# Graph attention network on one core: one StreamTranspose and four small writes for a row, three of four masked tiles scaled by ScalarE, the last batches in halves, and a new order of steps

## The chip, the cores and the metric

The kernel runs on one core of a Trainium2 chip. The core has five engines that work side by side: TensorE (PE, matmuls and transposes), VectorE (DVE), ScalarE (ACT), GpSimd (POOL) and SyncE (SP, which here only starts DMAs). Each takes its instructions in the order in which the program gives them, and waits at semaphores. The metric is the time of one execution on the device, in microseconds.

## The reference, cut to what matters

x has 16 batches of 512 nodes with 128 features; adj is a 512 x 512 matrix of edges. Two blocks follow one another, the first with two attention layers, the second with one:

```
def gat(inp, adj_mask, W, a):
    h = inp @ W
    f1, f2 = h @ a[:F, 0], h @ a[F:, 0]
    e = leaky_relu(f1[:, :, None] + f2[:, None, :], 0.2)
    e = where(adj_mask > 0, e, -9e15)        # not in the first layer
    return elu(softmax(e, axis=2) @ h)

h = relu(layernorm(x))                       # 16 x 512 x 128
o = relu(h @ mlp1_w + mlp1_b)                # 256 wide
o = elu(gat(o, None, W_fc, a_fc)) + o        # layer 1, 256 wide, no mask
o = relu(o @ mlp2_w + mlp2_b)                # 128 wide
o = relu(elu(gat(o, adj, W_hand, a_hand)) + o)   # layer 2, masked
x = x + o
h = relu(layernorm(x))
x = x + elu(attention(h, adj, W, a) @ (h @ W))   # layer 3, masked
```

## The kernel before, in words

A batch is cut into four tiles (C = 4) of 128 nodes. For each batch, numbered 0 to 15, the kernel does the same chain of steps, and each step has a name: `load`, `stats1`, `root1`, `norm1`, `turn1` (layer norm and transposing), `mlp1_0`, `mlp1_1`, `h1_0` to `h1_3`, `max1`, `args1`, `row1`, `prob1_0` to `prob1_3`, `att1_0` to `att1_3`, `elu1_0`, `elu1_1`, `z_0`, `z_1` (layer 1), `mlp2`, then the masked layer 2 (`h2`, `max2`, `args2`, `row2`, `prob2`, `att2`, `elu2`, `turn_o2`, `x1`, `norm2`, `root2`, `turn2`) and the masked layer 3 (`h3`, `max3`, `args3`, `row3`, `prob3`, `att3`, `elu3`, `result`). Step `x1` makes the residual x + o, `norm2` its statistics and normalised tiles, which `turn2` on TensorE transposes for `h3`.

The softmax's weights are never computed as an exponential of a sum over 512 x 512 pairs. exp(leaky_relu(f1 + f2)) is the larger of two products, so ScalarE takes exponentials of three short columns (`args`, L728, into `square`), and an attention tile is max(row x scale, bound), then cut by the mask with a minimum. For that, one of the columns (one value for each of the 512 nodes) has to lie along the free axis and be the same on all 128 partitions: the *row*. In batches 0 to 2 and 13 to 15 (which of them depends on the layer) TensorE spreads it by transposing a broadcast column and ScalarE copies it (L735). In the other 36 cases VectorE transposes the 128 x 32 tile `square` in four blocks of 32 x 32 into `square_t` with 32 partitions (`turn_row`, L1019), SyncE writes four lines of 512 B to DRAM (L570), waits for that, and loads the row broadcast to 128 partitions (L580).

The attention tiles of a masked layer are made in `prob_alone` and `prob_scaled`. VectorE makes tiles 0 and 1 alone, with a TensorScalar each (multiply, max; L1041) and then a TensorTensor each (min with the mask; L1046). For tiles 2 and 3 ScalarE multiplies the row (L744), and VectorE takes max and min in one ScalarTensorTensor (L1053). The attention's matmuls on TensorE (L1281 for layer 1, L1364 for the masked ones) wait for these tiles; a reciprocal on VectorE (L1090, L1097) and a scaled copy on ScalarE (L775, L785) read their bank. elu is an Exp on ScalarE (L793; twice in layers 1 and 2, L797) and a ScalarTensorTensor on VectorE (L1105); `x1` is two more (L954, L961), `result` one (L1120), each of 512 columns.

What each engine does when is written out by hand: `ORDER` holds for each of the five engines the list of its steps with their batches, and several batches are under way at once in different layers. Matmuls go through eight banks of PSUM in turn, in TensorE's order, so a matmul also waits until the bank of eight fillings before has been read. Most buffers have two slots, for even and odd batches. At the end a general version of the network stands behind a flag (`guard`, `flag`), which runs only where the scores leave a range; it does not run with these inputs.

Of the kernel before, what the change touches and what calls it, by code (L numbers as in the profile page):

```python
# [6 lines left out]
P = 128  # L7
# [12 lines left out]

WARM = (10, 12)
# [7 lines left out]
        load.0 load.1 weights load.2 load.3 load.4 load_again.0 load.5 load.6 load.7 load.8 load.9 row1.3  # L29
        load_again.1 load.10 row1.4 row1.5 load.11 row2.2 load_again.2 row2.3 load.12 row3.1 result.0 load.13  # L30
        row1.6 row2.4 load_again.3 row1.7 row2.5 load.14 row3.2 row3.3 load_again.4 result.1 load.15 row1.8
        row2.6 load_again.5 row1.9 row2.7 row3.4 row1.10 row3.5 result.2 load_again.6 result.3 result.4
        load_again.7 load_again.8 result.5 row2.8 row3.6 row3.7 row1.11 row2.9 load_again.9 result.6 row2.10
        load_again.10 row1.12 result.7 row3.8 row2.11 row1.13 row3.9 load_again.11 result.8 row1.14 row3.10
        row2.12 result.9 load_again.12 row3.11 row1.15 load_again.13 result.10 result.11 row3.12 load_again.14
        load_again.15 result.12 result.13 result.14 result.15
    """,
    "gpsimd": """
        max1.0 max1.1 max1.2 max2.0 max1.3 max2.1 max1.4 max3.0 max1.5 max2.2 max2.3 max3.1 max1.6 max2.4
        max1.7 max2.5 max3.2 max3.3 max1.8 max2.6 max2.7 max1.9 max3.4 max1.10 max3.5 max2.8 max3.6 max2.9  # L40
        max3.7 max1.11 max2.10 max1.12 max3.8 max2.11 max3.9 max1.13 max1.14 max3.10 max2.12 max2.13 max3.11
        max1.15 max2.14 max3.12 max3.13 max2.15 max3.14 max3.15 guard
    """,
    "scalar": """
        weights root1.0 turn_w1 turn_w23 root1.1 turn1.0 turn1.1 root1.2 mlp1_0.0 mlp1_1.0 h1_0.0 h1_1.0
        mlp1_0.1 h1_2.0 root1.3 h1_3.0 turn1.2 mlp1_1.1 turn1.3 h1_0.1 h1_1.1 mlp1_0.2 h1_2.1 args1.0 h1_3.1
        root1.4 masks_0 mlp1_1.2 masks_1 row1.0 args1.1 masks_2 masks_3 root1.5 row1.1 att1_0.0 att1_1.0
        elu1_0.0 turn1.4 att1_2.0 root1.6 h1_0.2 h1_1.2 att1_3.0 elu1_1.0 h1_2.2 h1_3.2 att1_0.1 att1_1.1
        turn1.5 mlp1_0.3 root1.7 elu1_0.1 mlp1_1.3 att1_2.1 mlp2.0 att1_3.1 h2_0.0 root1.8 args1.2 h2_1.0
        h1_0.3 elu1_1.1 h1_1.3 h1_2.3 args2.0 h1_3.3 args1.3 row2.0 prob2_2.0 row1.2 mlp2.1 prob2_3.0 h2_0.1  # L50
        mlp1_0.4 att2_0.0 turn1.6 att2_1.0 elu2.0 h2_1.1 root1.9 mlp1_1.4 att1_0.2 args2.1 att1_1.2 row2.1
        elu1_0.2 h1_0.4 prob2_2.1 prob2_3.1 att1_2.2 root1.10 root2.0 h1_1.4 h1_2.4 h1_3.4 turn2.0 args1.4
        att1_3.2 elu1_1.2 att2_0.1 att1_0.3 att2_1.1 att1_1.3 h3_0.0 elu2.1 elu1_0.3 att1_2.3 att1_3.3 elu1_1.3
        h3_1.0 att1_0.4 args3.0 mlp1_0.5 mlp1_1.5 row3.0 att1_1.4 h1_0.5 root2.1 h1_1.5 prob3_2.0 prob3_3.0
        elu1_0.4 mlp1_0.6 h1_2.5 h1_3.5 att1_2.4 args1.5 att1_3.4 mlp2.2 turn2.1 elu1_1.4 mlp2.3 turn1.7 h3_0.1
        h2_0.2 h2_1.2 args2.2 att1_0.5 h2_0.3 mlp2.4 h2_1.3 att1_1.5 elu1_0.5 att1_2.5 args2.3 att1_3.5 h3_1.1
        prob2_2.2 elu1_1.5 att3_0.0 mlp1_1.6 turn1.8 att3_1.0 prob2_3.2 root1.11 args3.1 mlp1_0.7 prob2_2.3
        elu3.0 h1_0.6 h1_1.6 h1_2.6 h1_3.6 prob2_3.3 mlp2.5 turn1.9 mlp1_1.7 att2_0.2 mlp1_0.8 prob3_2.1
        prob3_3.1 h2_0.4 h1_0.7 args1.6 h2_1.4 att2_1.2 h1_1.7 h1_2.7 root1.12 elu2.2 args2.4 h1_3.7 args1.7
        root2.2 att3_0.1 att3_1.1 turn2.2 att2_0.3 h2_0.5 att2_1.3 h2_1.5 prob2_2.4 args2.5 prob2_3.4 elu2.3  # L60
        elu3.1 att1_0.6 h3_0.2 att1_1.6 elu1_0.6 prob2_2.5 att2_0.4 att1_2.6 mlp1_1.8 prob2_3.5 att2_1.4
        att1_3.6 turn1.10 h1_0.8 h3_1.2 h1_1.8 elu2.4 elu1_1.6 turn2.3 root2.3 args3.2 att2_0.5 h1_2.8 att2_1.5
        h3_0.3 h3_1.3 att1_0.7 att1_1.7 prob3_2.2 root1.13 args3.3 mlp1_0.9 h1_3.8 mlp2.6 elu2.5 elu1_0.7
# [1419 lines left out]
```

## Time and profile before

| | us |
|---|---|
| time, median of 3 runs | 476.24 (475.93 to 479.42) |
| the profiled execution: its own time | 479.25 |
| the profiled execution: its span, first to last instruction | 477.5 |
| TensorE busy | 435.4 (91%), 2601 matmuls |
| VectorE busy | 387.4 (81%), 1371 instructions |
| ScalarE busy | 306.8 (64%), 739 instructions |
| GpSimd busy | 26.6 (6%) |
| mean granted TensorE clock | 0.984 of full speed |

Busy time is the time in which at least one instruction of the engine runs; the rest of the span it waits. Where an engine had been idle, the profile names what released it.

### The profile page before, as it was taken

How to read it: one execution, taken by the hardware profiler on the slowest of the kernel's cores; microseconds unless marked ns; L12 is line 12 of the kernel's file. 1: busy time of each engine (PE TensorE's matmuls, PEld its weight loads, DVE VectorE, ACT ScalarE, POOL GpSimd, SP SyncE). 2: the span in 40 equal slices, each digit the busy share in tenths (PEclk: the TensorE clock that was granted, in tenths of full speed). 3: DMA queues.
4: the chain of work that ended last, by engine and by line, in shares of the span. 5: the costliest groups of instructions: out<-in, count | busy, mean ns of one | idle time of the engine just before them, and what ended most of it. 6: DMA issues, size and time to landing. Idle time of an engine off the chain costs nothing. (4 is left out here: it accounts for less than half of the span.)

```text
span 477.5 us, 8672 instructions
## 1 busy us (share of the span) xinstructions
PE 435.4 (91%) x2601; PEld 366.6 (77%) x2601; DVE 387.4 (81%) x1371; ACT 306.8 (64%) x739; POOL 26.6 (6%) x53
## 2 busy tenths in 40 slices
PE   6899999999999899999989998999899997978582
PEld 6678778877779787878878867888788896967472
DVE  6796588586699988799998886997896999888862
ACT  2566747757477486947676863886746594866552
POOL 0000000000001000010000010001001000100000
PEclk9999999999999999999999998999999999999977
DMA  6210120001122201230132022102210303020001
GB/s 209 67 46 23 45 66 1 25 0 44 46 68 67 68 24 44 68 85 19 53 110 71 22 69 66 46 22 68 77 34 25 88 1 84 29 68 22 23 1 49
DMA packets 32394, 24.42 MB, mean 51 GB/s; under 512 B 1595, under 2 KB 27222, under 8 KB 32342
## 3 DMA queue, kind: packets, MB, share of 16 engines
q1 hardware_dynamic: 30960, 22.23, 16.1%
q10 hardware_dynamic: 1382, 1.58, 1.0%
q8 instruction: 22, 0.36, 0.3%
q14 instruction: 30, 0.25, 0.2%
HBM read 19.54 MB, written 4.27 MB: 50 GB/s over the span
## 5 line engine op out<-in xcount | busy, mean ns | idle before, releaser
L1364 PE MATMUL bank<-ext,prob 128*128 128x129 f32 x1024 | 129.4, 280 | 7.4 <-DVE prob L1053 6.1
L1364 PEld LDWEIGHTS bank<-ext,prob 128*128 128x128 f32 x1024 | 123.6, 194 | 15.0 <-DVE prob L1053 8.8
L1281 PE MATMUL bank<-ext,prob 128*128 128x257 f32 x512 | 118.1, 381 | 2.3 <-DVE prob L1031 2.0
L1281 PEld LDWEIGHTS bank<-ext,prob 128*128 128x128 f32 x512 | 94.6, 190 | 18.8 <-issue 3.7
L1270 PE MATMUL bank<-wfc_sb,o_t 128*128 128x259 f32 x256 | 64.1, 386 | 1.3 <-ACT o_t L682 1.3
L1270 PEld LDWEIGHTS bank<-wfc_sb,o_t 128*128 128x128 f32 x256 | 46.8, 193 | 10.1 <-issue 2.9
L1105 DVE SCALAR_TENSOR_TENSOR u<-e,y 128x512 f32<-128x512 f32 x64 | 43.8, 688 | 11.7 <-ACT e L797 7.3
L785 ACT ACTIVATE y<-bank,recip 128x128 f32<-128x128 f32 x128 | 39.0, 369 | 21.5 <-DVE recip L1097 20.6
L609 POOL PARTITION_ALL_REDUCE fmax<-fmax_col x48 | 26.0, 545 | 432.2 <-DVE fmax_col L983 432.2
L775 ACT ACTIVATE y<-bank,recip 128x256 f32<-128x256 f32 x64 | 29.8, 474 | 30.9 <-DVE recip L1090 30.3
L1053 DVE SCALAR_TENSOR_TENSOR prob<-prob,square,mask_t 128x512 f32<-128x512 f32 x64 | 47.0, 746 | 2.7 <-ACT prob L744 2.5
L793 ACT ACTIVATE e<-y,minus_one 128x512 f32<-128x512 f32 x64 | 46.3, 724 | 0.9
L744 ACT ACTIVATE prob<-row,square 128x512 f32<-128x512 f32 x64 | 44.7, 724 | 0.9 <-DMA row<-row_scratch 0.7
L1046 DVE TENSOR_TENSOR prob<-prob,mask_t 128x512 f32<-128x512 f32 x64 | 41.3, 688 | 0.0
L1041 DVE TENSOR_SCALAR prob<-row,square 128x512 f32<-128x512 f32 x64 | 32.0, 544 | 4.9 <-ACT row L735 4.7
L797 ACT ACTIVATE e<-e,minus_one 128x512 f32<-128x512 f32 x48 | 34.8, 724 | 1.6
L1019 DVE STREAM_TRANSPOSE square_t<-square 32x32 f32<-32x32 f32 x144 | 28.6, 198 | 7.1 <-ACT square L728 3.4
L690 ACT ACTIVATE ext<-bank 128x259 f32<-128x259 f32 x64 | 23.3, 386 | 16.4 <-PE bank L1270 15.5
L1031 DVE TENSOR_SCALAR prob<-row,square 128x512 f32<-128x512 f32 x64 | 32.4, 540 | 1.6 <-DMA row<-row_scratch 1.5
L1299 PE MATMUL bank<-z_t,w_sb 128*128 128x512 f32 x64 | 30.6, 600 | 2.2 <-DVE z_t L1112 1.5
L1261 PE MATMUL bank<-normed_t,w_sb 128*128 128x512 f32 x64 | 32.0, 596 | 0.4 <-ACT y L785 0.4
L728 ACT ACTIVATE square<-args 128x12 f32<-128x12 f32 x48 | 10.1, 210 | 32.8 <-DVE args L1004 17.8
(95 smaller groups left out, 535.0 us busy)
## 6 DMA issues: line engine op xcount, KB each, us to landing
row<-row_scratch SPq DMA_DIRECT2D x36, 256.0 KB, 3.2
x_in<-in_x SPq DMA_DIRECT2D x16, 256.0 KB, 2.8
x_res<-in_x SPq DMA_DIRECT2D x16, 256.0 KB, 4.1
out<-y_out SPq DMA_DIRECT2D x16, 256.0 KB, 2.8
adj_sb<-in_adj ACTq DMA_DIRECT2D x1, 1024.0 KB, 5.5
row_scratch<-square_t SPq DMA_DIRECT2D x36, 2.0 KB
wfc_sb<-in_L_gnn_W_fc ACTq DMA_DIRECT2D x1, 256.0 KB, 3.8
w_sb<-in_L_gnn_mlp_w SPq DMA_DIRECT2D x1, 128.0 KB, 4.0
```

The costliest lines, as they stand in the source:

```text
L744: nc.scalar.activation(L.prob_of(b)[:, t], L.row[:, b.slot], ACT.Copy, scale=L.buv[:, b.slot, 2, t:t + 1]).then_inc(s.scaled_row.sem, 1)
L785: nc.scalar.activation(L.y[:, c], filled[:, e * (D + 3):e * (D + 3) + D], ACT.Copy, bias=1.0, scale=L.recip[:, b.slot, c:c + 1]).then_inc( ...
L793: nc.scalar.activation(L.e[:, r], L.y[:, r], ACT.Exp, bias=minus_one[:]).then_inc(s.exp.sem, 1)
L797: nc.scalar.activation(L.e[:, r], L.e[:, r], ACT.Exp, bias=minus_one[:]).then_inc(s.exp2.sem, 1)
L1031: nc.vector.tensor_scalar(gat1.prob_of(b)[:, t], gat1.row[:, b.slot], gat1.buv[:, b.slot, 2, t:t + 1], gat1.buv[:, b.slot, 1, t:t + 1], AL ...
L1041: nc.vector.tensor_scalar(p[:, t], L.row[:, b.slot], L.buv[:, b.slot, 2, t:t + 1], L.buv[:, b.slot, 1, t:t + 1], ALU.mult, ALU.max).then_i ...
L1046: nc.vector.tensor_tensor(p[:, t], p[:, t], mask_t[:, t], ALU.min).then_inc(s.prob_ready.sem, 1)
L1053: nc.vector.scalar_tensor_tensor(out=p, in0=p, scalar=L.buv[:, b.slot, 1, t:t + 1], in1=mask_t[:, t], op0=ALU.max, op1=ALU.min).then_inc(s ...
L1105: nc.vector.scalar_tensor_tensor(out=L.u[:, r], in0=L.e[:, r], scalar=1.0, in1=L.y[:, r], op0=ALU.min, op1=ALU.max).then_inc(s.u.sem, 1)
L1270: last = nc.tensor.matmul(filled[:, 0:H + 3], o1_t[:, b.of(O1_DEPTH), k, c * P:(c + 1) * P], wfc_sb[:, k], start=(k == 0), stop=(k == HT - 1))
L1281: last = nc.tensor.matmul(filled[:, 0:H + 1], gat1.targets(b, t, c), gat1.features_and_one(b, t), start=(t == 0), stop=(t == C - 1))
L1364: last = nc.tensor.matmul(filled[:, e * (D + 3):e * (D + 3) + D + 1], L.targets(b, t, c), L.features_and_one(b, t), start=(t == 0), stop=( ...
```

## The change

1. `turn_row` issues one StreamTranspose of the whole 128 x 32 tile. It turns each block of 32 x 32 where it stands, so the four lines of the row no longer lie on partitions 0 to 3 with 512 B each, but in four groups of partitions with 128 B for each line. SyncE writes them with four DMAs, one for each group, issued one after the other.
2. In the masked layers VectorE makes only tile 0 alone (`ALONE = 1`); ScalarE multiplies the row for tiles 1, 2 and 3, and VectorE follows with one instruction each.
3. For batches 13, 14 and 15 `elu2`, `x1`, `norm2`, `elu3` and `result` are done in halves of two tiles, on ScalarE and VectorE, and `turn2` on TensorE waits for the first two normalised tiles before its first transposes and for the others in the middle. The semaphores count two per batch. The store still waits for both halves.
4. The lists of `ORDER` are new for all five engines. TensorE's 407 steps are the same, as are the batches whose row TensorE spreads; ScalarE's list has 601 steps for 563 and VectorE's 672 for 625.

The diff without most of the lists:

```diff
+ALONE = 1
+HALVED = (13, 14, 15)
 ORDER = {
     "scalar": """
-        weights root1.0 turn_w1 turn_w23 root1.1 turn1.0 turn1.1 root1.2 mlp1_0.0 mlp1_1.0 h1_0.0 h1_1.0
-        mlp1_0.1 h1_2.0 root1.3 h1_3.0 turn1.2 mlp1_1.1 turn1.3 h1_0.1 h1_1.1 mlp1_0.2 h1_2.1 args1.0 h1_3.1
+        weights root1.0 root1.1 turn_w1 turn1.0 turn1.1 mlp1_0.0 root1.2 mlp1_1.0 h1_0.0 turn_w23 root1.3
+        h1_1.0 mlp1_0.1 h1_2.0 h1_3.0 mlp1_1.1 turn1.2 h1_0.1 root1.4 h1_1.1 h1_2.1 mlp1_0.2 turn1.3 args1.0
...
     "vector": """
-        constants stats1.0 vectors norm1.0 ones stats1.1 norm1.1 scores1 stats1.2 norm1.2 edges stats1.3 max1.0
+        constants stats1.0 stats1.1 norm1.0 norm1.1 ones vectors stats1.2 scores1 norm1.2 stats1.3 norm1.3
...
-        norm2.1 prob3_0.0 z_1.3 prob3_2.0 root2n.1 att1_2.4 elu1_0.4 max1.5 args1.5 att1_3.4 row1.5 norm1.9
-        elu1_1.4 z_0.4 z_1.4 max2.2 prob1_0.5 prob1_1.5 args2.2 prob1_2.5 row2.2 stats1.11 prob1_3.5 att1_0.5
+        elu1_1.3 att1_1.4 stats1.10 att1_2.4 norm1.9 z_0.3 max1.5 z_1.3 root2n.1 args1.5 row1.5 elu1_0.4
+        att1_3.4 elu1_1.4 z_0.4 z_1.4 max3.1 prob1_0.5 prob1_1.5 args3.1 max2.2 prob1_2.5 row3.1 prob1_3.5
...
-        x1.15 max3.14 norm2.15 args3.14 root2n.15 prob3_0.14 prob3_2.14 max3.15 prob3_3.14 args3.15 att3_0.14
-        prob3_0.15 prob3_2.15 prob3_3.15 att3_1.14 guard elu3.14 att3_0.15 att3_1.15 result.14 elu3.15
-        result.15 flag
+        att2_0.15 prob3_3.14 elu3_0.13 att2_1.15 result_0.13 elu3_1.13 elu2_0.15 result_1.13 x1_0.15 elu2_1.15
+        att3_0.14 norm2_0.15 x1_1.15 norm2_1.15 root2n.15 max3.15 elu3_0.14 args3.15 att3_1.14 prob3_0.15
+        prob3_1.15 prob3_2.15 prob3_3.15 guard result_0.14 att3_0.15 elu3_1.14 result_1.14 flag att3_1.15
+        elu3_0.15 result_0.15 elu3_1.15 result_1.15
...
     "tensor": """
-        warm_0 vectors turn_w1 turn_w23 warm_1 turn1.0 scores1 mlp1_0.0 turn1.1 mlp1_1.0 mlp1_0.1 mlp1_1.1 scores23 h1_0.0
+        warm_0 turn_w1 vectors warm_1 turn1.0 turn1.1 scores1 mlp1_0.0 mlp1_1.0 mlp1_0.1 turn_w23 mlp1_1.1
...
-                self.square_t = sb(f"square_t{k}", [32, 2, P])
+                self.square_t = sb(f"square_t{k}", [P, 2, 32])
...
             def write_row(b, L):
                 s = sig[L]
-                sp.wait_ge(*s.turned.at(b, C))
+                sp.wait_ge(*s.turned.at(b, 1))
...
-                sp.dma_start(L.scratch[b.slot].rearrange("(c p) -> c p", c=C),
-                             L.square_t[0:C, b.slot]).then_inc(s.row_written.sem(b), 16)
+                rows = L.scratch[b.slot].rearrange("(c k i) -> k c i", c=C, k=ROWS)
+                for k in range(ROWS):
+                    sp.dma_start(rows[k], L.square_t[32 * k:32 * k + C, b.slot]).then_inc(s.row_written.sem(b), 16)
...
             def scale_row(b, L, t):
                 s = sig[L]
-                if t == C // 2:
+                if t == ALONE:
                     act.wait_ge(*s.row_loaded.landed(b))
...
+            def residual2(b, part, parts):
+                done = (part + 1) * 2 // parts
                 r = slice(part * C // parts, (part + 1) * C // parts)
+                dve.wait_ge(*s2.u.at(b, done))
                 dve.wait_ge(*o2n_filled.at(b, 1))
+                nc.vector.scalar_tensor_tensor(
+                    out=gat2.u[:, r], in0=bank_of("turn_o2", b)[:].rearrange("p (c n) -> p c n", c=C)[:, r], scalar=-1.0,
+                    in1=gat2.u[:, r], op0=ALU.add, op1=ALU.add).then_inc(v_ready.sem, 2 // parts)
...
+            def norm2(b, part, parts):
 
+                tiles = range(part * C // parts, (part + 1) * C // parts)
+                dve.wait_ge(*x1_ready.at(b, (part + 1) * 2 // parts))
...
-                for k in range(C):
-                    nc.vector.transpose(L.square_t[:, b.slot, 32 * k:32 * (k + 1)],
-                                        L.square[32 * k:32 * (k + 1), b.slot]).then_inc(s.turned.sem, 1)
+                nc.vector.transpose(L.square_t[:, b.slot], L.square[:, b.slot]).then_inc(s.turned.sem, 1)
...
-                for t in range(C // 2):
+                for t in range(ALONE):
                     nc.vector.tensor_scalar(p[:, t], L.row[:, b.slot], L.buv[:, b.slot, 2, t:t + 1],
                                             L.buv[:, b.slot, 1, t:t + 1], ALU.mult, ALU.max).then_inc(
                         s.unmasked.sem, 1)
-                for t in range(C // 2):
+                for t in range(ALONE):
                     dve.wait_ge(*s.unmasked.at(b, t + 1))
                     nc.vector.tensor_tensor(p[:, t], p[:, t], mask_t[:, t], ALU.min).then_inc(s.prob_ready.sem, 1)
...
             def turn2(b):
-                pe.wait_ge(*normed_ready[1].at(b, C))
+                parts = 2 if not general and b.n in HALVED else 1
+                pe.wait_ge(*normed_ready[1].at(b, C // parts))
                 filled = free("turn2", b)
                 for c in range(C):
+                    if parts == 2 and c == C // 2:
+                        pe.wait_ge(*normed_ready[1].at(b, C))
                     last = nc.tensor.transpose(filled[:, c * P:(c + 1) * P], normed[1][:, b.slot, c], ident[:])
```

## Rows read from the trace of the kernel before

**Rows 1.** The page: busy us (share of the span) x instructions of each engine.
```profile
PE 435.4 (91%) x2601; PEld 366.6 (77%) x2601; DVE 387.4 (81%) x1371; ACT 306.8 (64%) x739; POOL 26.6 (6%) x53
```

**Rows 2.** Four stretches: length, busy of PE, PEld, DVE, ACT, POOL; clock, DMA, GB/s.
```profile
0.00:20.00 20.00, 15.82 (x71) 12.86 (x72) 13.58 (x85) 7.65 (x17) 0.19 (x4) 1.00 0.52 164
20.00:420.00 400.00, 382.68 (x2285) 321.89 (x2285) 334.39 (x1165) 266.87 (x646) 23.29 (x44) 1.00 0.17 48
420.00:469.20 49.20, 36.86 (x248) 31.87 (x247) 37.24 (x117) 30.96 (x74) 3.10 (x5) 0.93 0.10 28
469.20:477.50 8.30, 0.00 (x0) 0.00 (x0) 2.23 (x5) 1.35 (x3) 0.00 (x0) 0.69 0.24 71
```

**Rows 3.** Waits of TensorE from 20 to 420 us: total us, times, longest.
```profile
PE bank L1364 <- DVE prob L1053: 4.6, 5, 2.0
PE bank L1281 <- DVE prob L1031: 2.0, 3, 0.7
...
PE bank L1243 <- DVE prob L902: 0.2, 1, 0.2
```

**Rows 4.** Groups by line and shape: busy us, mean ns, idle before.
```profile
L1053 DVE SCALAR_TENSOR_TENSOR prob<-prob,square,mask_t 128x512 f32<-128x512 f32 x64 | 47.0, 746 | 2.7 <-ACT prob L744 2.5
L744 ACT ACTIVATE prob<-row,square 128x512 f32<-128x512 f32 x64 | 44.7, 724 | 0.9 <-DMA row<-row_scratch 0.7
L1046 DVE TENSOR_TENSOR prob<-prob,mask_t 128x512 f32<-128x512 f32 x64 | 41.3, 688 | 0.0
L1041 DVE TENSOR_SCALAR prob<-row,square 128x512 f32<-128x512 f32 x64 | 32.0, 544 | 4.9 <-ACT row L735 4.7
L1019 DVE STREAM_TRANSPOSE square_t<-square 32x32 f32<-32x32 f32 x144 | 28.6, 198 | 7.1 <-ACT square L728 3.4
L853 DVE STREAM_TRANSPOSE lane_t<-lane 128x32 f32<-128x32 f32 x1 | 0.2, 211 | 0.0
```

**Rows 5.** Row 1.5 in order of time (start us, us), and the landing of all rows.
```profile
112.31 0.89 DVE L1019 STREAM_TRANSPOSE square_t<-square 32x32 f32<-32x32 f32 x4 [0.20 <-ACT square L728]
113.23 0.26 SPq L570 DMA_DIRECT2D row_scratch<-square_t  x1
114.41 0.33 SPq L580 DMA_DIRECT2D row<-row_scratch  x1
119.51 1.03 DVE L1031 TENSOR_SCALAR prob<-row,square 128x512 f32<-128x512 f32 x2
...
DMA to landing us min/median/max: 3.0/3.2/4.3
```

**Rows 6.** The head's timeline: two starts of TensorE after a wait, and ScalarE's turn1.2.
```profile
6.58 0.25 PE L1198 MATMUL bank<-ident,vec_sb 11*128 11x11 f32 x1 [0.61 <-DMA vec_sb<-in_L_gnn_mlp_b]
...
21.12 0.60 ACT L667 ACTIVATE normed_t<-bank 128x512 f32<-128x512 f32 x1
...
22.34 2.02 PE L1270 MATMUL bank<-wfc_sb,o_t 128*128 128x259 f32 x8 [1.27 <-ACT o_t L682]
```

**Rows 7.** Groups by line and shape: wide and narrow forms of the halved operations.
```profile
L1105 DVE SCALAR_TENSOR_TENSOR u<-e,y 128x512 f32<-128x512 f32 x64 | 43.8, 688 | 11.7 <-ACT e L797 7.3 <-ACT e L793 2.5 <-PE bank L1289 1.6
...
L793 ACT ACTIVATE e<-y,minus_one 128x512 f32<-128x512 f32 x64 | 46.3, 724 | 0.9
...
L657 ACT ACTIVATE log_var<-meanvar,ln_eps 128x4 f32<-128x4 f32 x32 | 9.5, 298 | 12.7 <-DVE meanvar L919 12.6
...
L1004 DVE SCALAR_TENSOR_TENSOR args<-args,empty_arg 128x4 f32<-128x4 f32 x32 | 5.2, 163 | 1.1
```

**Rows 8.** The tail's timeline: batch 15's normalised tiles, and the last result.
```profile
451.26 0.87 DVE L974 TENSOR_SCALAR normed<-x,meanvar 128x128 f32<-128x128 f32 x4
...
452.19 1.11 PE L1332 MATMUL bank<-ident,normed 128*128 128x128 f32 x4 [4.17 <-DVE normed L974]
...
471.58 0.69 DVE L1120 SCALAR_TENSOR_TENSOR y_out<-u,x 128x512 f32<-128x512 f32 x1
```

**Rows 9.** Who waited for the rows' load: us, times.
```profile
  DVE prob L1031: 1.5, 1
```

More of the change, by code:

```diff
@@ L28 @@
     "sync": """
[L29 to L33, printed above, removed]
@@ L34 @@
-        load_again.10 row1.12 result.7 row3.8 row2.11 row1.13 row3.9 load_again.11 result.8 row1.14 row3.10
-        row2.12 result.9 load_again.12 row3.11 row1.15 load_again.13 result.10 result.11 row3.12 load_again.14
-        load_again.15 result.12 result.13 result.14 result.15
+        load.0 load.1 weights load.2 load.3 load.4 load_again.0 load.5 load.6 load_again.1 load.7 load.8 load.9
+        row1.3 row1.4 load.10 row1.5 row3.1 row2.2 row2.3 load_again.2 load.11 load.12 row2.4 row2.5 row3.2
@@ new lines @@
+        row1.6 load_again.3 load_again.4 load.13 result.0 row1.7 load_again.5 load.14 row1.8 row3.3 result.1
+        row2.6 row2.7 load.15 row3.4 row1.9 row3.5 result.2 load_again.6 load_again.7 row1.10 load_again.8
+        result.3 result.4 load_again.9 row3.6 row2.8 row3.7 row2.9 row1.11 result.5 row2.10 row1.12
+        load_again.10 load_again.11 result.6 row3.8 row3.9 row2.11 result.7 row1.13 result.8 row3.10 row2.12
+        load_again.12 row1.14 row3.11 row1.15 row3.12 result.9 result.10 load_again.13 load_again.14
@@ L37 @@
+        load_again.15 result.11 result.12 result.13 result.14 result.15
     """,
     "gpsimd": """
[L39 to L42, printed above, removed]
+        max1.0 max1.1 max1.2 max2.0 max1.3 max2.1 max1.4 max3.0 max1.5 max3.1 max2.2 max2.3 max2.4 max2.5
@@ L47 @@
[L47 to L51, printed above, removed]
@@ L252, in landed @@
     def landed(self, b):
-        return self.sems[b.slot], (b.half + (self.before(b) + 1)) * 16
+        return self.sems[b.slot], (b.half + (self.before(b) + 1)) * 16 * self.parts
     def two_back(self, b):
-        return self.sems[b.slot], (b.half + self.before(b)) * 16
+        return self.sems[b.slot], (b.half + self.before(b)) * 16 * self.parts
 def gnn_program(nc, x, adj, w1, b1, w2, b2, wfc, afc, whand, ahand, wl1, al1, out):
@@ L408, in signal, with slots @@
             return Signal(semaphore(name), per_batch, skipped, without)
-        def slots(name, without=()):
-            return SlotSignal([semaphore(f"{name}{k}") for k in range(2)], without)
+        def slots(name, without=(), parts=1):
+            return SlotSignal([semaphore(f"{name}{k}") for k in range(2)], without, parts)
         waited = {name: semaphore(f"waited_{name}") for name in ("dve", "pool", "sp")}
```

378 lines of the change are left out of this document (197 added, 181 removed), and 4 rows, old and new, of the table lock_step.

## The prediction

> **What bounds the kernel now.** I read the page first: of the span of 477.5 us TensorE is busy for 91%, VectorE for 81%, ScalarE for 64% [rows 1]. Then the busy times of four stretches [rows 2], to see where TensorE is *not* busy. It idles 20.0 - 15.8 = 4.2 us in the first 20 us, 400 - 382.7 = 17.3 us in the long middle, 49.2 - 36.9 = 12.3 us from 420 us to its last matmul, and it has nothing to do in the last 8.3 us. That is 42 us in all, and since the change leaves every matmul as it is (the same 407 tensor steps in another order), no rearrangement can return more than that: TensorE's 435.4 busy us stay.
>
> The third view, who TensorE waited for in the middle, splits the 17.3 us [rows 3]: seven rows name VectorE as the releaser, 11.7 us together (the prob tiles lead with 4.6 and 2.0), eight name ScalarE, 5.4 us together. So VectorE, the second-busiest engine, holds TensorE up twice as much as ScalarE. That is the money on the table in the middle; the rest of VectorE's time is hidden behind matmuls.
>
> **The turned row.** Four StreamTransposes of 32x32 take 198 ns each; the trace has one of 128x32, in the constants, at 211 ns [rows 4]. So 36 rows (those not spread by TensorE) save 4 x 198 - 211 = 581 ns each, 20.9 us of VectorE, all of it before 420 us. In exchange SyncE issues four small writes for one: an issue holds its queue 0.26 us, and the row's load is issued 1.18 us after the write's issue [rows 5]. Three more issues add 0.78 us, and 0.58 us of that comes back from the shorter transpose, so a row arrives 0.2 us later. Whether writes of 128 B complete more slowly than of 512 B the trace can't show; the bounds are nothing and, four in a queue each with its own wait of 1.18 us, 4 x 1.18 - 1.18 - 0.78 = 2.8 us more. I take nothing, since the writes are issued without a wait between them. Queued behind them on SyncE are loads of x and stores of results, which are needed many us later; 36 x 0.78 = 28 us of issue on a queue that mostly waits for VectorE costs nothing by itself.
>
> **The second masked tile goes to ScalarE.** Each of the 32 masked preparations drops one 544 ns TensorScalar and one 688 ns TensorTensor and gains a 746 ns ScalarTensorTensor: 486 ns less of VectorE, 15.6 us in all, against a 698 ns copy (44.7 / 64) more on ScalarE, 22.3 us in all [rows 4]. 27 of the 32 lie before 420 us. Cover for ScalarE's extra work is its 36% idle time.
>
> **The middle, summed.** VectorE's 334.4 us there fall by 20.9 + 27 x 0.486 = 13.1 to 300.4: its idle share rises from 16.4% to 24.9%. ScalarE's 266.9 rise by 27 x 0.698 = 18.8 to 285.7: its idle share falls from 33.3% to 28.6% [rows 2]. I let TensorE's waits on an engine shrink or grow inversely with that engine's idle share: 11.7 x 16.4 / 24.9 = 7.7 (4.0 less), 5.4 x 33.3 / 28.6 = 6.3 (0.9 more). Middle: **-3.1 us**. This is a choice; the bounds are -11.7 (all waits on VectorE go) and nothing or a loss (below).
>
> **The head.** TensorE waited 0.61 us for the vectors' DMA with the weights' turn queued behind; now turn_w1 stands first. Later it waited 1.27 us for an o_t tile whose copy stood on ScalarE behind the copy of turn1.2 (a 0.6 us instruction); these two change places [rows 6]. I take 0.6 + 0.4 = **-1.0 us**, between nothing and -1.9. The early norm1.1 only feeds matmuls that already stand without a gap. The masks' fourth tile is put off to where prob2 needs it, also in a stretch without gaps: nothing.
>
> **The tail.** VectorE's busy time does not fall here: five prob preparations save 5 x 0.49 = 2.4 us, and halving costs about as much. An instruction of 256 columns is in no row of this form; interpolated between 4 columns (163 ns) and 512 (688 ns) it is 0.42 us on VectorE, and between 298 and 724 ns 0.51 us on ScalarE [rows 7]. Two halves so cost 0.16 us more than a whole on VectorE (15 of them, 2.4 us) and 0.29 on ScalarE (9, 2.6 us). The bounds of a half are half of the whole (0.34) and the whole (0.69). What halving gains is latency, since the first half runs while TensorE still attends to the second: after the last sum of a batch, each exp is 0.215 us shorter and each ScalarTensorTensor 0.265.
> - x1.15: TensorE waits 4.17 us for this batch's normalised tiles, its longest wait [rows 8]. Two exps, three ScalarTensorTensors and half of the 0.87 us of normalising give 0.43 + 0.80 + 0.43 = 1.7 us. Bounds: nothing, if VectorE, 76% busy there, is still at an older half; 4.17 at most.
> - The last three masked preparations of the trace (prob2.15, prob3.14, prob3.15) stand on the path. Before, row to last tile is two TensorScalars, two TensorTensors, two ScalarTensorTensors, 3.5 us; now one, one and three, 3.3 us: -0.26 each, -0.8.
> - The end: exp, elu and result in halves, -0.215 - 2 x 0.265 = -0.75 of what follows the last matmul [rows 8]. The guard's flag moves ahead of it at no gain, since the store outlasts it.
>
> Tail: **-3.2 us**. Sum: -3.1 - 1.0 - 3.2 = -7.3 us on the profiled execution's 479.25 us, so 471.9 for it. That execution is 3.0 us above the median of the runs, 476.24; the edits don't touch what makes runs differ, so I put the same -7.3 on the median: **468.9 us**.
>
> **The rivals.** A measurement of this kernel tells about 1% from no change, 471.5 to 481.0 us.
>
> *The relief is hidden* (21%). VectorE idled 66 us in the middle already, and the long tables of steps fix who waits in which place; the new order may put as many waits elsewhere. For it: PE's waits are few and scattered (15 rows), each decided by the order and not by load. Against: they do name VectorE, and the one on prob comes right behind VectorE's work. Then only the vectors' 0.6, the end's 0.75 and the probs' 0.8 are left: 474.1 us, the same.
>
> *More than the sum* (12%). With VectorE at 75% nothing of the 11.7 us is left, the head gives 1.9, and in the tail the whole wait of 4.17 goes beside 0.75 + 0.8: 476.2 - 19.3 = 456.9 us.
>
> *The rows come late* (13%), the slower side. From the write's issue a row needs 1.18 + 0.78 + 3.2 (median landing) = 5.2 us before its prob can start [rows 5]. Adding up VectorE's own work between a row's transposes and its first prob, by the steps of the new order and the durations of the rows, I find 14 of the 36 rows with less than that (the worst, row1.5, with 2.8), 8.9 us short in sum; at the slowest landing, 4.3 us, 16 rows and 25 us short. In the old order, by the same count at 4.4 us, it was 3 rows and 3.6 us, of which the trace shows 1.5 as VectorE's wait [rows 9]. And now both VectorE and, with three tiles to scale instead of two, ScalarE stand still for a late row, with bank copies queued behind. It decides once over 7 us of such waits reach TensorE. With half of the 25 us reaching it, the middle's relief lost, and head and tail as above: 476.2 - 4.2 + 12.5 = 484.5 us. Against it: VectorE also waits for TensorE between those steps (row1.5's prob started 6.3 us after its transposes, where its bare work is 3.6), so most shortfalls are filled by waits that exist anyway. The Trainium skill speaks for this rival: "DMA: Bandwidth & Descriptors" (Specifications, and Rules for kernel authors) says that pieces under 512 B are written by read-modify-write and that many small transfers should be coalesced, and this change does the opposite. Its fixed cost of about 2.0 us for a DMA is not what the trace shows for this write (1.18 us to the next issue); by the page's figure the row would come 0.8 us later still, in both kernels.
>
> **How the numbers follow.** My forecast has 54%, at 468.9 us, its own range 464 to 474 (head from nothing, middle from -1 to -7). About four fifths of it lies below 471.5, so faster by over 1%: 0.54 x 0.8 + 0.12 = 0.55, and a part of the hidden case is near the border, 0.07 more: 0.62. Within 1%: 0.11 + 0.14 = 0.25. Slower: 0.13. The range leaves out the ends of the two extreme rivals: 459 to 478 us.
>
> **What would show it.** In the profile after: StreamTranspose 128x32 x36 near 211 ns; ScalarE's prob group x96 and TensorTensor x32; VectorE near 353 us busy, ScalarE near 332, TensorE still near 435. Right, if TensorE's idle time from 20 to 420 us is near 14 us with fewer waits on prob, and if under 8 us lie between the last matmul and the end. Late rows would show as ScalarE's or VectorE's idle time released by the row's DMA, above 5 us. I'd be wrong if TensorE's waits on ScalarE (o_t, ext, y copies) grow by more than those on VectorE shrink, or if the halves queue up behind one another on VectorE and the wait before the last normalised tiles stays at 4 us.

## The result, and the profile after

The changed kernel takes 452.45 us (median of 4 runs, 451.98 to 454.53) against 476.22: a ratio of 0.9495 with a 95% interval of 0.9445 to 0.9545, 23.8 us less. The forecast was 7.3 us less: the sign was right, the size a third of what came, and the time lies 6.5 us below the range. The profiled executions differ by more than the medians, 477.5 - 450.2 = 27.3 us of span, because that of the kernel before was one of its slowest (479.25 us).

The page of the kernel after: span, and busy us (share) x instructions of each engine, as [rows 1].

```profile
span 450.2 us, 8759 instructions
PE 425.7 (95%) x2601; PEld 363.4 (81%) x2601; DVE 356.5 (79%) x1246; ACT 326.0 (72%) x780; POOL 25.0 (6%) x53
```

VectorE lost 387.4 - 356.5 = 30.9 us (34 forecast), ScalarE gained 19.2 (25). But TensorE, whose 2601 matmuls are the same, is also busy for 9.7 us less than in [rows 1]. I had called its 435.4 us a floor.

Three stretches of the kernel after, columns as in [rows 2]:

```profile
0.00:20.00 20.00, 15.10 (x73) 11.72 (x73) 13.87 (x91) 8.53 (x21) 0.19 (x4) 1.00 0.56 165
20.00:395.00 375.00, 373.15 (x2270) 318.16 (x2270) 301.80 (x1022) 281.74 (x671) 22.82 (x44) 1.00 0.18 52
395.00:450.20 55.20, 37.44 (x259) 33.48 (x258) 40.81 (x134) 35.75 (x91) 1.96 (x5) 0.89 0.10 31
```

And the kernel after over the middle stretch of [rows 2], where the forecast was that TensorE would still idle near 14 us; it idles 6.2:

```profile
20.00:420.00 400.00, 393.79 (x2410) 336.56 (x2411) 325.27 (x1100) 302.02 (x723) 23.87 (x47) 0.99 0.18 51
```

And the middle one of the kernel before, cut at the same 395 us:

```profile
20.00:395.00 375.00, 360.19 (x2131) 301.87 (x2130) 312.04 (x1095) 251.59 (x610) 21.58 (x42) 1.00 0.16 48
```

In these 375 us TensorE idled 14.8 us before and 1.9 after, and it got 2270 matmuls done instead of 2131. The granted clock is 1.00 in both. Those 139 matmuls, at 375 / 2270 = 0.165 us each, are 23 us of progress, of which 13 us were visible as idle time. The rest had been inside "busy". This row of the kernel after shows how:

```profile
418.51 5.53 PE L1390 MATMUL bank<-ext,prob 128*128 128x129 f32 x48
```

48 matmuls in a row take 5.53 us. One is recorded as 0.28 us long (mean of its group; the profile models the ends of matmuls), so they start (5.53 - 0.28) / 47 = 0.112 us apart. A stall that holds the next start back by less than 0.28 - 0.112 = 0.17 us leaves no idle time at all, and of a longer one 0.17 us is missing.

So I took from both traces the distances between the starts of matmuls, with the median distance of each line of the kernel as its time when nothing holds it up, and called what lies above the median a stall:

| us | before | after |
|---|---|---|
| ahead of the first matmul | 3.6 | 3.6 |
| 2600 distances at the median of their line | 414.4 | 414.2 |
| stalls, what the distances hold above it | 50.9 | 25.4 |
| from the last matmul's start to the end | 8.5 | 6.9 |

The floor was near 414 us and the stalls 51 us, not 435 and the 30 us of idle time that [rows 2] shows from the first matmul to the last. Some 5 us of the stalls in either trace are no waits but matmuls in stretches with the granted clock at 1.2 GHz instead of 2.4. From 20 to 395 us the stalls fell from 27.2 us to 5.3.

Who TensorE waited for in the kernel after (whole span; total us, times, longest):

```profile
PE bank L1358 <- DVE normed L994: 4.7, 4, 1.8
PE bank L1215 <- DVE ident L875: 3.6, 1, 3.6
PE bank L1332 <- ACT square L744: 2.9, 1, 2.9
PE bank L1390 <- DVE prob L1064: 2.1, 1, 2.1
...
PE bank L1390 <- DVE prob L1071: 0.5, 3, 0.2
```

Of the prob waits of [rows 3] (4.6 and 2.0 us between 20 and 420 us) 0.2 us is left, and from 20 to 395 us TensorE idles 1.9 us in all.

### The profile page after: what moved, and what is told of

Its sections match the earlier page's. It is cut to its first block, busy times and chain, and to the rows that moved or that the text cites. A ratio compares the mean times of both kernels' runs of the same rounds, so it can differ in the third digit from the quotient of the medians.

```text
span 450.2 us, 8759 instructions
## 1 busy us (share of the span) xinstructions
PE 425.7 (95%) x2601; PEld 363.4 (81%) x2601; DVE 356.5 (79%) x1246; ACT 326.0 (72%) x780; POOL 25.0 (6%) x53
## 3 DMA queue, kind: packets, MB, share of 16 engines
q1 hardware_dynamic: 31824, 22.23, 17.3%
## 4 chain that ended last, share of the span: by engine, by line
PE 60%; DVE 4%; ACT 2%; issue 2%; DVEq 0%; ACTq 0%
PE bank L1390 20%; PE bank L1304 15%; PE bank L1293 8%; PE bank L1340 5%; PE bank L1322 3%; PE bank L1284 3%; PE bank L1312 2%; PE bank L1358 1%; PE bank L1398 1%; DVE stats L930 1%; ACT prob L760 1%; PE bank L1276 1%; DVE u L971 1%; DVE u L1123 1%; ACT y L801 1%
## 5 line engine op out<-in xcount | busy, mean ns | idle before, releaser
L1390 PE MATMUL bank<-ext,prob 128*128 128x129 f32 x1024 | 125.9, 278 | 2.8 <-DVE prob L1064 2.1
L1071 DVE SCALAR_TENSOR_TENSOR prob<-prob,square,mask_t 128x512 f32<-128x512 f32 x96 | 69.0, 741 | 3.7 <-ACT prob L760 3.6
L760 ACT ACTIVATE prob<-row,square 128x512 f32<-128x512 f32 x96 | 66.1, 717 | 2.4 <-DMA row<-row_scratch 2.3
L1123 DVE SCALAR_TENSOR_TENSOR u<-e,y 128x512 f32<-128x512 f32 (+1 forms) x70 | 44.5, 639 | 17.7 <-ACT e L813 14.0
L809 ACT ACTIVATE e<-y,minus_one 128x512 f32<-128x512 f32 (+1 forms) x70 | 47.8, 684 | 1.3
L1049 DVE TENSOR_SCALAR prob<-row,square 128x512 f32<-128x512 f32 x64 | 32.9, 540 | 6.1 <-ACT row L751 3.2
L813 ACT ACTIVATE e<-e,minus_one 128x512 f32<-128x512 f32 (+1 forms) x51 | 35.5, 697 | 2.4
L698 ACT ACTIVATE o_t<-bank,b_sb 128x512 f32<-128x512 f32 x32 | 21.7, 684 | 12.7 <-PE bank L1284 10.9
L734 ACT ACTIVATE ext<-bank,rstd 128x131 f32<-128x131 f32 x64 | 19.6, 373 | 10.6 <-PE bank L1340 7.2
L1340 PEld LDWEIGHTS bank<-wl_sb,normed_t 128*128 128x128 f32 x128 | 18.5, 207 | 6.3 <-ACT normed_t L689 4.0
```

Source lines behind the costliest of these rows:

```text
L760: nc.scalar.activation(L.prob_of(b)[:, t], L.row[:, b.slot], ACT.Copy, scale=L.buv[:, b.slot, 2, t:t + 1]).then_inc(s.scaled_row.sem, 1)
L809: nc.scalar.activation(L.e[:, r], L.y[:, r], ACT.Exp, bias=minus_one[:]).then_inc(s.exp.sem, 2 // parts)
L813: nc.scalar.activation(L.e[:, r], L.e[:, r], ACT.Exp, bias=minus_one[:]).then_inc(s.exp2.sem, 2 // parts)
L1071: nc.vector.scalar_tensor_tensor(out=p, in0=p, scalar=L.buv[:, b.slot, 1, t:t + 1], in1=mask_t[:, t], op0=ALU.max, op1=ALU.min).then_inc(s ...
L1123: nc.vector.scalar_tensor_tensor(out=L.u[:, r], in0=L.e[:, r], scalar=1.0, in1=L.y[:, r], op0=ALU.min, op1=ALU.max).then_inc(s.u.sem, 2 // ...
L1340: last = nc.tensor.matmul(filled[:, e * (D + 3):(e + 1) * (D + 3)], src[:, c * P:(c + 1) * P], L.w[:, 0], start=True, stop=True)
```

## The experiments

Sixteen kernels ran. Medians of the kernel before were 478.0, 477.8, 477.4 and 478.0 us in the four groups, so a difference below 2 us between groups isn't read as one. A ratio is to the kernel before of the same group, with its 95% interval. All sixteen are made from the code of the changed kernel, with the operations of before put back where a run needs them; a step that isn't halved has the instructions of before and counts two at its semaphore.

### The edits apart, in the old and in the new order

**old_order_all_edits**: the changed kernel with the lists of before.

```diff
-HALVED = (13, 14, 15)
+HALVED = ()
 ORDER = {   # the lists of before, with
-        ... prob2_0.2 ...            (vector)
+        ... prob2_0.2 prob2_1.2 ...
-        ... prob2_2.2 ...            (scalar)
+        ... prob2_1.2 prob2_2.2 ...
```

> The single transpose with four small writes and the three scaled tiles, in the order of before (the new second-tile step stands right behind tile 0 on VectorE and right ahead of tile 2 on ScalarE), nothing in halves. Theory A (the order makes the gain: the freed VectorE time is worth little as long as each engine's list was laid out for the old durations): 471 us or more, above three quarters of the gain missing, TensorE still over 10 us idle between 20 and 420 us. Theory B (the freed time itself makes it, the list only follows): 456 to 462 us, idle there under 6 us.

470.47 us, 0.9851 (0.9799 to 0.9903). That is 7.5 us less than before, half a microsecond under theory A's 471, and two thirds of the gain are missing, not three quarters. From 20 to 395 us there are 2167 matmuls and 12.3 us of idle time, to 420 us 14.3, as theory A had it. The -7.5 us look like my -7.3; the runs below show that they are something else.

**new_order_alone**: the new lists with the old operations (the one write of a row too, which this excerpt leaves out).

```diff
-ALONE = 1
+ALONE = 2
-HALVED = (13, 14, 15)
+HALVED = ()
-                nc.vector.transpose(L.square_t[:, b.slot], L.square[:, b.slot]).then_inc(s.turned.sem, 1)
+                for k in range(C):
+                    nc.vector.transpose(L.square_t[:, b.slot, 32 * k:32 * (k + 1)],
+                                        L.square[32 * k:32 * (k + 1), b.slot]).then_inc(s.turned.sem, 1)
```

> The new order with the old operations: four transposes and one write, two tiles made by VectorE alone, nothing in halves (a halved step stands where its second half stood). Theory A (the order makes the gain): 455 to 461 us, since VectorE at 84% of the shorter span still fits. Theory B (the freed 34 us of VectorE make it): VectorE falls behind in the lists that count on shorter steps, 468 us or more. A third theory, both are needed and neither alone gives a third of the 23.8 us: 468 us or more here and in the run of all edits in the old order.

485.27 us, 1.0145 (1.0094 to 1.0196): 1.5% slower, clear of the noise though under 2%. Theory A falls, the order alone makes nothing. Theory B had fallen with the run above. The third one is nearest, but its numbers, 468 or more in both, hide that the order alone is a loss. More than half of this loss is not in the middle: the 2200th matmul starts 2.8 us later than in the kernel before (397.3 and 394.5 us), and from there to the end it takes 87.0 us instead of 83.0.

**old_order_row**: lists of before, `ALONE = 2`, no halves, single transpose and four writes.

> Only the single transpose and four small writes, in the order of before. VectorE loses 21 us of work. Theory A: 473 to 477 us. Theory B: half of its gain, 464 to 469 us. If a row that comes 1 us later matters (my rival): slower than before, 478 us or more, with waits on the row's load above 5 us.

465.65 us, 0.9744 (0.9698 to 0.9791): -12.4 us, half of the whole gain, in theory B's range, and better than all edits together in this order. The rival fell: waits on the row's load rose from 2.2 us to 4.6, and the run is still 12.4 us faster.

**old_order_scaled**: lists of before with prob_1 as above, `ALONE = 1`, four transposes and one write, no halves.

> Only the third scaled tile, in the order of before. VectorE loses 15 us, ScalarE gains 22. Theory A: 473 to 478 us. Theory B: 466 to 471 us. If ScalarE's copies of banks are pushed back enough to hold TensorE: 479 us or more, with TensorE's waits on o_t, ext and y above the 5.4 us of before.

481.75 us, 1.0085 (1.0053 to 1.0116): a small loss, in the third case's range. Its sign is there too: from 20 to 420 us TensorE's waits on ScalarE grew from the 5.4 us of before to 7.5, and those on VectorE fell only from 11.7 to 10.9. ScalarE's prob group grew from 44.7 us [rows 4] to 64.2. VectorE's prob instructions of the masked layers went from 32.0 + 41.3 + 47.0 = 120.3 us [rows 4] to 109.2, so 11.1 us less, not 15.6:

```profile
L1069 DVE SCALAR_TENSOR_TENSOR prob<-prob,square,mask_t 128x512 f32<-128x512 f32 x96 | 69.7, 744 | 9.8 <-ACT prob L756 9.2
...
L1062 DVE TENSOR_TENSOR prob<-prob,mask_t 128x512 f32<-128x512 f32 x32 | 22.2, 692 | 1.1
L1057 DVE TENSOR_SCALAR prob<-row,square 128x512 f32<-128x512 f32 x32 | 17.3, 541 | 3.9 <-ACT row L747 3.8
```

The idle column of its first row explains more: VectorE waits 9.2 us for ScalarE's scaled tiles, where it waited 2.5 us in [rows 4]. VectorE's busy time in the whole span fell only 8.8 us.

The same two edits in the new order, again without halves:

> The new order with the single transpose and four writes, but two tiles made by VectorE alone and nothing in halves. Theory F (in either order the freed VectorE time is what counts, and the list of steps says how much of it arrives): 485.3 us of the new order alone less 15 to 20 for the row, 465 to 470 us. Rival R (the row edit is worth 12 us in any order, and the rest comes from the scaled tile in its new places): 472 to 474 us.

468.83 us, 0.9823 (0.9767 to 0.9879): 16.4 less than the new order alone. Theory F.

> The new order with three scaled tiles, but four transposes and one write for a row and nothing in halves. Theory F: 15 us less of VectorE where the list expects them gone: 485.3 less 10 to 15, 470 to 475 us. Rival (scaling a third tile costs here what it cost in the old order, 3.7 us): 485 us or more.

474.51 us, 0.9947 (0.992 to 0.9973): 10.8 less than the new order alone. The same edit that lost 3.7 us in the old lists. VectorE's wait for ScalarE's tiles is 2.9 us here, against 9.2 in the old lists, where tile 1's copy stands right ahead of tile 2's; that the places in the lists make this difference is the natural reading, not tested by itself.

> The changed kernel without the halves (each halved step stands whole where its second half stood). Theory L (the halves shorten only the last chain): 454 to 457 us, 2 to 4 us above the changed kernel, all of it after the 2200th matmul. Rival: the halves are worth nothing because VectorE is full there, 452 to 453.5 us.

460.05 us, 0.9631 (0.9575 to 0.9687). The halves are worth 7.6 us, about twice the most that theory L allowed; that all of it comes after the 2200th matmul was right. Medians in us, without halves:

| | neither edit | row | scaled tile | both |
|---|---|---|---|---|
| lists of before | 478.0 (the kernel before) | 465.7 | 481.8 | 470.5 |
| new lists | 485.3 | 468.8 | 474.5 | 460.1 |

Each edit is worth more in the new lists, most of all the scaled tile (from +3.7 to -10.8), and the new lists pay only once VectorE has less to do: +7.3 without the edits, -10.4 with both.

### The halves

The middle of the run without halves is that of the changed kernel (373.34 us busy, 2273 matmuls). Its timeline behind 400 us has these starts of TensorE after a wait:

```profile
409.90 1.25 PE L1328 MATMUL bank<-ident,square 128*128 128x128 f32 x8 [3.74 <-ACT square L740]
413.34 1.12 PE L1354 MATMUL bank<-ident,normed 128*128 128x128 f32 x4 [2.19 <-DVE normed L990]
...
433.82 1.12 PE L1354 MATMUL bank<-ident,normed 128*128 128x128 f32 x4 [4.90 <-DVE normed L990]
```

With halves the same places read:

```profile
409.54 1.09 PE L1332 MATMUL bank<-ident,square 128*128 128x128 f32 x8 [2.93 <-ACT square L744]
...
411.48 0.69 PE L1358 MATMUL bank<-ident,normed 128*128 128x128 f32 x2 [0.58 <-DVE normed L994]
...
428.04 0.44 PE L1358 MATMUL bank<-ident,normed 128*128 128x128 f32 x2 [1.78 <-DVE normed L994]
...
430.16 0.44 PE L1358 MATMUL bank<-ident,normed 128*128 128x128 f32 x2 [1.68 <-DVE normed L994]
```

The waits for the normalised tiles (L1354, L1358) got shorter twice. For batch 14 they went from 2.19 us to 0.58, and for batch 15 one wait of 4.90 us became two, ahead of either half, of 1.78 and 1.68. Batch 13's had no wait in either run. The granted clock from 395 us to the end is 0.89 instead of 0.79, and the matmuls there keep TensorE for 37.4 us instead of 40.4. From 395 us on the changed kernel needs 55.2 us, the one without halves 63.1.

TensorE's lists are the same in the two runs, so each matmul can be compared with itself. The lead of the halves over the profiled run without them is -0.5 us at the 2421st, 2.3 behind batch 14's normalised tiles (the 2441st), 4.2 behind batch 15's (the 2541st), 6.6 at the last and 7.9 at the end of the span. The 2.4 us between the last two matmuls named lie where the run without halves has the granted clock at 1.2 GHz for longer (431 to 441 and 445 to 448 us, against 431 to 435 us). What the clock alone is worth wasn't separated by a run.

**old_order_row_halves**: the old lists with the row edit and each halved step as two in the place of one.

> The order of before with the single transpose and with the halves (both halves where the whole step stood; on ScalarE the first exp right behind the first sums). Beside the run with the row alone in the old order (465.7 us): Theory L: 462 to 464 us. Rival (halves cost instructions and gain nothing unless the steps between them are placed anew): 465.5 to 467.5 us.

469.06 us, but from 464.65 to 469.53; 0.9793 (0.972 to 0.9866) against 0.9744 (0.9698 to 0.9791) without halves. The intervals overlap: no gain is shown, and a loss isn't either, and the time is above both ranges. Halves that stand back to back on VectorE don't help measurably; whether they harm stays open. The one execution of 464.65 us had a mean granted clock of 0.987, the three slower ones 0.976 to 0.977.

### What the single transpose took away: load, or lateness of the row

**new_padded** and **new_padded_8**: spare transposes behind the real one. **old_order_row_padded** and **old_order_row_padded_8**: the same on old_order_row.

```diff
                 nc.vector.transpose(L.square_t[:, b.slot], L.square[:, b.slot]).then_inc(s.turned.sem, 1)
+                for k in range(0 if general else 3):      # 8 in the second pair
+                    nc.vector.transpose(pad_t[:, L.k, b.slot, k], lane[:])
```

> The changed kernel, and behind each of the 36 single transposes three more StreamTransposes of 128x32 into a tile that nobody reads: VectorE gets its 21 us back, but the row isn't later. Theory V (VectorE's load is what the single transpose took away): 462 to 468 us, as the removed edit (14 us in the new order without halves). Theory C (the row's chain got shorter, the load is hidden): 452 to 455 us.

> The same padding on the single transpose in the order of before (465.7 us without it). Theory V: 475 to 479 us, back at the kernel before. Theory C: 465 to 468 us.

457.34 us, 0.957 (0.9528 to 0.9611), and 467.12 us, 0.9775 (0.9732 to 0.9819): neither theory's range in the first, theory C's in the second. The page explains it: VectorE was busy for 365.2 us in the first, only 8.7 more than without, because spare transposes to tiles that nobody reads overlap and add 0.08 us each, where the four real ones of [rows 5] took 0.89 us together. The dose was too small.

> The changed kernel with eight spare StreamTransposes behind each real one. Three spare ones cost VectorE only 0.24 us for a row (8.7 us busy in all, +4.9 us of time); eight should cost 0.65 us, the whole that the edit removed (23 us). Theory V (load): about 13 us slower than the changed kernel, 463 to 468 us. Theory C (the load is mostly hidden, and the three spare ones just hit a bad place): 456 to 460 us.

> The same eight spare ones on the single transpose in the order of before (465.7 us without, 467.1 with three). Theory V: back at the kernel before, 474 to 478 us. Theory C (here something other than the load gave the 12 us): 466 to 470 us.

466.02 us, 0.976 (0.97 to 0.982), and 476.09 us, 0.9967 (0.994 to 0.9995): theory V in both. The pages of new_padded_8 and, below it, old_order_row_padded_8:

```profile
PE 432.4 (93%) x2601; PEld 364.8 (79%) x2601; DVE 380.7 (82%) x1534; ACT 326.6 (70%) x780; POOL 23.9 (5%) x53
```

```profile
PE 432.1 (91%) x2601; PEld 363.4 (77%) x2601; DVE 388.8 (82%) x1551; ACT 305.9 (65%) x739; POOL 27.0 (6%) x53
```

In the new order 24.2 us more of VectorE cost 13.6 us, in the old one 24.1 cost 10.4. So what the single transpose took away was for the most part VectorE's load: 0.43 to 0.56 us of time for each us. The time came back almost to the kernel before (476.09 and 477.98 us) with all the row's writes and transposes left in their new form. The slope isn't one number: the three spare ones cost 4.9 us for 8.7 in the new order, as steep as the eight, but 1.5 us for 8.8 in the old one. And the scaled tile's 10.8 us in the new order, for 9.9 us less of VectorE, are more than any of these slopes gives; why isn't shown.

**new_row_later** and **old_order_row_later**: four more small writes to a place that nobody reads, which the row's load also waits for.

```diff
+                for k in range(ROWS):
+                    sp.dma_start(spare[k], L.square_t[32 * k:32 * k + C, b.slot]).then_inc(s.row_written.sem(b), 16)
```

> The changed kernel with eight small writes for a row instead of four (four go to a place that nobody reads), which holds each of the 36 rows back by about 1.3 us more and adds nothing to any engine but SyncE. My rival that late rows cost: 3 us or more slower than the changed kernel, 455.5 us or more, with waits on the row's load growing from 6 us to over 15. Theory V (there is slack between the row and its use): 452 to 454 us.

> Single transpose and eight small writes for a row in the order of before: each row 1.4 us later. In the new order that cost 11.3 us. If the old lists leave the row more room (3 rows short by my count against 14): under 4 us here, 466 to 469 us. If a late row costs as much in either order: 475 to 479 us.

463.78 us, 0.9721 (0.9679 to 0.9762), and 480.93 us, 1.0068 (1.0033 to 1.0104). SyncE's timeline of new_row_later, one row:

```profile
107.10 1.26 SPq L589 DMA_DIRECT2D row_scratch<-square_t  x4
108.41 1.31 SPq L591 DMA_DIRECT2D row_spare<-square_t  x4
110.60 0.34 SPq L600 DMA_DIRECT2D row<-row_scratch  x1
```

From the first write to the load's issue it is 3.5 us there (median of 36), 2.15 in the changed kernel and 1.18 before [rows 5]. The extra 1.4 us cost 11.3 us in the new order and 15.3 in the old, above even the higher of its two ranges; the expectation that the old lists leave more room fell. Waits on the row's load grew from 4.6 to 38.2 us in the old order and from 6.4 to 28.4 us in the new:

```profile
DVE prob L1063 <- DMA row<-row_scratch: 11.4, 10, 2.2
ACT prob L764 <- DMA row<-row_scratch: 10.2, 9, 3.3
DVE prob L1053 <- DMA row<-row_scratch: 6.8, 6, 3.6
```

**new_row_two_queues**: two of the four writes by GpSimd, in whose list each row stands as it does in VectorE's.

```diff
-                for k in range(ROWS):
+                for k in range(ROWS - 2):
                     sp.dma_start(rows[k], ...)
+            def write_half_row(b, L):
+                pool.wait_ge(*s.turned.at(b, 1))
+                for k in range(ROWS - 2, ROWS):
+                    pool.dma_start(rows[k], L.square_t[32 * k:32 * k + C, b.slot]).then_inc(
+                        s.row_written_pool.sem(b), 16)
```

> The changed kernel with two of the four small writes of a row issued by GpSimd, so that SyncE issues two. If late rows still cost in the changed kernel and GpSimd's writes land as fast: the load is issued up to 0.6 us sooner, 448 to 451 us. If GpSimd's writes take longer than the two issues they save: slower, 455 us or more, with the gap from first write to load above 2.2 us.

453.47 us, 0.9492 (0.9445 to 0.9539), as the changed kernel. SyncE issues two writes in 0.59 us, but GpSimd's take 1.03 us and start 0.3 us later, and in the profiled execution the load is issued 2.67 us after the first write (median), 0.5 later than with four writes by SyncE. That gap is what the second expectation named, but its 455 us or more didn't come. The row didn't come sooner, so this run doesn't say what a sooner row is worth; that its half a microsecond more cost nothing here, where 1.4 us cost 11, is not explained.

**new_store_halves**: the last two results stored in two DMAs each, to see if the end gets shorter.

```diff
+                    sp.wait_ge(*y_ready.at(b, 1))
+                    sp.dma_start(out_v[b.n][:, 0:2], y_out[:, b.slot, 0:2]).then_inc(s_half, 16)
                     sp.wait_ge(*y_ready.at(b, 2))
+                    sp.dma_start(out_v[b.n][:, 2:4], y_out[:, b.slot, 2:4]).then_inc(stored.sem(b), 16)
```

> The changed kernel, but the results of batches 14 and 15 are stored in two DMAs of 128 KB, the first as soon as its half is made. After the last result 256 KB take 3.4 us to the end of the span; if the size of the last DMA matters: 0.3 to 0.8 us faster, 451.7 to 452.2 us. If the landing is all fixed cost: the same, 452.4 us.

453.27 us (451.23 to 456.42), 0.9512 (0.9469 to 0.9554): the same. No version tried beats the changed kernel.

## Why the prediction was wrong

**"TensorE's 435.4 busy us stay"** is the first step that failed. It made 42 us the most that could be won, and 17.3 us the most in the middle. Busy time of pipelined matmuls contains up to 0.17 us of each of their stalls. The stalls were 51 us, and some 25 of them went: 16 that showed as idle time and 9.7 out of the busy time.

**The middle, -3.1 us**, is the step that carries the miss. Cut at the start of the 200th and of the 2200th of the 2601 matmuls, the profiled executions differ by -1.1 us in the head (47.3 to 46.2 us), -19.2 in the middle (347.2 to 328.0) and -7.0 behind it (83.0 to 76.0), where I had -1.0, -3.1 and -3.2. I let waits shrink in proportion to an engine's idle share; the trace shows 14.8 us of idle time between 20 and 395 us turned into 1.9, and about 9 more behind the busy time.

The runs put two causes in its place. Load: a microsecond of VectorE's work costs about half a microsecond of time in either order, by the eight spare transposes, although VectorE idled 19% of the time. The row edit alone, 22.7 us of VectorE less, is -12.4 us in the old lists, -16.4 in the new. That this is so because the lists run many batches' chains through VectorE, and a late step delays all that follow on each engine, is my reading and not shown by a run. Placement: I priced the order at the head and the tail only. With both edits it is -10.4 us, spread over the run: in the changed kernel the 800th matmul starts at 152.4 us against 157.1 with all edits in the old order, the 1600th at 280.9 against 290.1, the 2200th at 374.2 against 387.6. Which of the moved steps do it stays open.

**The row.** "581 ns each, 20.9 us of VectorE" was nearly right (22.7), as was the 0.2 us later for a row (0.3: from the transpose to the load's issue 2.4 us against 2.1). The new transpose lasts 207 ns:

```profile
L1038 DVE STREAM_TRANSPOSE square_t<-square 128x32 f32<-128x32 f32 x36 | 7.4, 207 | 4.7 <-ACT square L744 4.4
```

By the runs with eight writes such lateness costs some 2 or 3 us in all; this is worked out from their slope and not shown by itself.

**The scaled tile.** 15.6 us less of VectorE was 11 to 12 in the prob instructions, as I took the mean durations of instructions that overlap their neighbours, and 8.8 to 9.9 in its whole busy time; ScalarE's 22.3 was 19.5 to 21.4. "Cover is its 36% idle time" was wrong for the old lists, where the edit lost 3.7 us and VectorE waited 9.2 us for the tiles; in the new ones it waited 2.9.

**The head, -1.0 us.** The two waits named went from 0.61 to nothing and from 1.27 to 0.71 us; two new ones of 0.36 and 0.90 us came before the first two `turn1`. So the waits named gave 1.17 us and the new ones took 1.26. That the 200th matmul starts 1.1 us sooner agrees with the number, but not by this sum, and since the lists differ it isn't the same matmul.

**The tail, -3.2 us.** Two of its three terms were right. From the last matmul's start to the last result it is 2.6 us instead of 3.35, the 0.75 of the forecast; a further 0.9 us went between the last result and the end of the span (5.2 to 4.3), which no term had and nothing here explains. The preparation of prob3.15, from row to last tile, takes 3.26 us instead of 3.53, the forecast's 0.26 less. Before, and below it after:

```profile
462.44 1.00 DVE L1041 TENSOR_SCALAR prob<-row,square 128x512 f32<-128x512 f32 x2 [1.36 <-ACT row L735]
463.36 1.29 DVE L1046 TENSOR_TENSOR prob<-prob,mask_t 128x512 f32<-128x512 f32 x2
464.56 1.41 DVE L1053 SCALAR_TENSOR_TENSOR prob<-prob,square,mask_t 128x512 f32<-128x512 f32 x2
```

```profile
437.05 0.55 DVE L1059 TENSOR_SCALAR prob<-row,square 128x512 f32<-128x512 f32 x1 [1.04 <-ACT row L751]
437.63 0.69 DVE L1064 TENSOR_TENSOR prob<-prob,mask_t 128x512 f32<-128x512 f32 x1
438.24 2.07 DVE L1071 SCALAR_TENSOR_TENSOR prob<-prob,square,mask_t 128x512 f32<-128x512 f32 x3
```

A half of 256 columns was forecast at 0.42 us on VectorE and 0.51 on ScalarE and measured so:

```profile
L809 ACT ACTIVATE e<-y,minus_one 128x256 f32<-128x256 f32 x12 | 6.1, 512 | 0.2
L1123 DVE SCALAR_TENSOR_TENSOR u<-e,y 128x256 f32<-128x256 f32 x12 | 5.0, 422 | 0.4 <-ACT e L809 0.4
```

The halves' worth was mis-sized: 1.7 + 0.75 us for them, 7.6 measured. The chain that I counted, that of x1.15, gave less than 1.7 by its waits: 4.17 us in the kernel before, 1.78 + 1.68 = 3.46 now (4.90 in the new lists without halves). But the chain of batch 14 was on the path as well, and with a granted clock that fell less the matmuls behind 395 us kept TensorE for 3 us less.

**The rivals.** *Hidden* was wrong. *More than the sum*, at 12%, was the case that came, and even it stopped at 456.9, since it took the visible waits for all there was. *Late rows* names a real price, 8 to 11 us of time for each us by which all rows are late, and the Trainium skill's rule in "DMA: Bandwidth & Descriptors" (Rules for kernel authors) to coalesce small transfers points the right way: the four writes hold SyncE for 1.26 us, the one for 0.26. But the row edit gained 12 to 16 us with that price paid. The sign that I had set for this rival, more than 5 us of waits on the row's load, came in the faster kernel all the same:

```profile
DVE prob L1049 <- DMA row<-row_scratch: 2.9, 1, 2.9
ACT prob L760 <- DMA row<-row_scratch: 2.3, 2, 1.5
DVE prob L1059 <- DMA row<-row_scratch: 1.2, 3, 0.6
```

So 6.4 us of such waits were no sign of a loss. The gap I had feared from short pieces on top of their issue isn't there: counted from the first write the load comes 2.15 - 1.18 = 0.97 us later, and the fourth write is issued 0.97 us after the first.

**Coincidence.** That all edits in the old order gave -7.5 us is no proof of my sum: it consists of -12.4 for the row and +4.8 for the scaled tile on top of it, which I had put at a part of -3.1 each, and it has neither the head's -1.0 nor the 1.7 + 0.75 us of the halves, since the lists and the steps in halves aren't in it.

## What to carry to other kernels

Take a pipelined engine's floor from the distance between the starts of back-to-back instructions, not from its busy time: every short stall is inside the latter. In a kernel whose engines run hand-laid lists, an engine that idles a fifth of its time still passes its delays on, so price load removed from the second-busiest engine by a slope (add a measured dose of work in the lists in question and see), and price an edit in the lists that it will run in, since the same edit can lose in one and gain in the other.

## What the runs showed of the hardware

- Spare StreamTransposes of 128x32 to tiles that nobody reads last 169 ns each but start 93 ns apart and add only 8.7 / 108 = 0.08 us each to VectorE's busy time; the four real ones of 32x32 took 0.89 us together, 0.22 each, at 198 ns each, and the one of 128x32 that does the same work 207 ns. A pad built from an operation costs what its overlap lets it.
- Four small DMAs of 4 x 128 B hold SyncE's queue for 1.26 us and are issued 0.30 to 0.34 us apart; two of them hold GpSimd's for 1.03 us.
